# A four-layer convolution kernel: the last layer's spline taps stacked on output partitions and gathered two chunks later

## The reference

```
patches = _extract_patches(_gn(x), KSIZE, STRIDE, PAD)      # 3x3 windows
bspl = _b_splines(patches, grid)                            # 8 cubic B-splines of every value
base_w = base_weight.sum(axis=2)
spl_w = (spline_weight * spline_scaler[..., None]).sum(axis=2)
out = einsum('bjhwn,ijn->bihw', silu(patches), base_w)
out = out + einsum('bjhwns,ijns->bihw', bspl, spl_w) + bias
x = x + out
```

## Time and profile before

| what | us |
|---|---|
| median of 3 runs (lowest, highest) | 12135.7 (12120.45, 12162.18) |
| the profiled execution, its own time | 12114.81 |
| its span, first to last instruction | 12112.6 |
| TensorE busy over the span | 9570.5 |
| VectorE busy | 8958.4 |
| ScalarE busy | 7397.5 |
| GpSimd busy | 5088.7 |

### The profile page before, as it was taken

One profiled execution on the slowest core, in us unless ns is written; L12 is line 12 of the kernel. 1 busy time (PEld: TensorE's weight loads), 2 busy tenths in 40 slices (PEclk: granted clock), 3 DMA queues, 4 the chain that ended last, 5 costly groups with the idle time before them and its releaser, 6 DMA issues. The chain is left out here.

```text
span 12112.6 us, 205123 instructions
## 1 busy us (share of the span) xinstructions
PE 9570.5 (79%) x53055; PEld 4412.5 (36%) x53055; DVE 8958.4 (74%) x10913; ACT 7397.5 (61%) x10963; POOL 5088.7 (42%) x2442
## 2 busy tenths in 40 slices
PE   0788578857886788640199999999999999997599
PEld 0566456645664566510022222222222222222233
DVE  1778487847784787637488888888888888887677
ACT  0455345534553455324288888888888888886354
POOL 0233133312321233100166666666666666665243
PEclk9899789977997799875599999999999999999799
DMA  2000100010000000004311111111111111112544
GB/s 86 1 0 0 28 8 0 0 29 7 0 0 21 15 0 0 37 28 143 98 29 29 29 27 25 28 29 29 29 29 29 29 29 27 28 26 54 130 115 100
DMA packets 227136, 410.60 MB, mean 34 GB/s; under 512 B 28784, under 2 KB 163024, under 8 KB 212336
## 3 DMA queue, kind: packets, MB, share of 16 engines
q1 hardware_dynamic: 226150, 399.26, 12.9%
HBM read 283.44 MB, written 115.70 MB: 33 GB/s over the span
## 5 line engine op out<-in xcount | busy, mean ns | idle before, releaser
L1194 POOL TENSOR_TENSOR l_a<-l_a 128x1018 f32<-128x1018 f32 x1851 | 3453.3, 1883 | 1687.8 <-ACT l_a L1339 1673.0
L1309 DVE TENSOR_TENSOR l_r<-l_pps,l_a 128x509 f32<-128x509 f32 x4755 | 2989.0, 677 | 46.0 <-PE l_pps L1208 28.1
L1333 ACT ACTIVATE l_a<-l_qps 128x509 f32<-128x509 f32 x3705 | 2155.3, 596 | 818.4 <-PE l_qps L1208 566.0
L1339 ACT ACTIVATE l_a<-l_a 128x1018 f32<-128x1018 f32 x2380 | 2504.0, 1052 | 40.3 <-issue 40.3
L1208 PE MATMUL l_qps<-l_mv,l_wst 123*128 123x509 bf16 x4235 | 1644.6, 388 | 170.1 <-ACT l_a L1333 50.0
L1208 PE MATMUL l_pps<-l_mv,l_wst 123*128 123x509 bf16 x4228 | 1624.4, 384 | 63.6 <-DVE l_r L1309 60.9
L652 POOL TENSOR_TENSOR a_pr<-a_pr 128x768 f32<-128x768 f32 x384 | 898.4, 2340 | 1639.1 <-DVE a_pr L567 1624.0
L681 ACT ACTIVATE a_g<-a_fps 128x512 f32<-128x512 f32 x1152 | 680.4, 597 | 998.7 <-PE a_fps L434 997.3
L434 PE MATMUL a_fps<-a_hbt,a_wfc 96*128 96x512 f32 x2304 | 1222.2, 666 | 70.2 <-ACT a_g L681 70.2
L452 POOL TENSOR_TENSOR a_pr<-a_qkv 128x768 f32<-128x768 f32 x128 | 386.6, 3039 | 2089.3 <-ACT a_qkv L694 2089.3
L1297 DVE TENSOR_SCALAR l_a<-l_qps 128x509 int32<-128x509 int32 x1058 | 724.5, 685 | 688.2 <-PE l_qps L1208 677.6
(11 more groups left out here) (162 smaller groups left out, 12030.2 us busy)
## 6 DMA issues: line engine op xcount, KB each, us to landing
l_mv<-pw SPq DMA_DIRECT2D x1608, 79.5 KB
l_gx<-g SPq DMA_DIRECT2D x66, 1040.0 KB
pw<-pw_hi SPq DMA_DIRECT2D x165, 127.2 KB
pw<-pw_mid SPq DMA_DIRECT2D x165, 127.2 KB
pw<-pw_lo SPq DMA_DIRECT2D x165, 127.2 KB
a_tb<-g SPq DMA_DIRECT2D x16, 1031.9 KB
l_x<-x SPq DMA_DIRECT2D x16, 1024.0 KB, 12.1
l_gs<-g SPq DMA_DIRECT2D x33, 260.0 KB
```

The source lines that it names most:

```text
L1194: g.tensor_tensor(a, a, a, ALU.mult).then_inc(sq_p, 2)
L1309: v.tensor_tensor(R[:, m % R_RING, :], pps[:, m % P_BANKS, 0:SUB], A[:, m % A_RING, :], ALU.mult).then_inc(mul_done, 1)
L1333: s_.activation(A[:, s % A_RING, :], qps[:, s % Q_BANKS, 0:SUB], ACT.Abs).then_inc(abs_a, 1)
L1339: s_.activation(a, a, ACT.Abs_reciprocal_sqrt, bias=1.0).then_inc(root_done, 2)
```

## The change

Only `layer3` and its constants change. TensorE makes for each chunk k and each image j first a plane (`multiply`): 64 output partitions for each parity hold the three vertical taps dy (16 channels each) stacked, the two parities side by side, summed over the three horizontal taps dx. ScalarE (j = 0, 2) and VectorE (j = 1, 3) copy the planes from PSUM to SBUF (`keep`). Two chunks later (`gather`) a constant matrix `pick` adds the rows of the planes, shifted by dy, into the output bank. Silu's rows are paired: partitions 64 and up of `gs` hold the row below, so that one matmul makes taps dy = 0 and 1, another dy = 2, each for one half of the images. The first clamp becomes a `Relu` on ScalarE right behind `Abs`, the second goes to GpSimd, and the last sum of the two cubes goes from GpSimd to VectorE. In SyncE's queue the one `gs` load becomes six smaller ones into a single slot, issued one chunk later and behind a wait for the silu before; stores come two chunks later, and a `gx` slot is reloaded when `bases` is counted.

```diff
-GX, BSLOTS = 3, 3
+GX, BSLOTS, PSLOTS, PBANKS = 3, 2, 3, 6
+HALF = 2
+KEEP_DVE = {1, 3}
...
-                            for b in range(NB):
-                                last = v.tensor_scalar(wba[:, :, b, :], sw[:, 0, :, :], mask[:, b:b + 1], None, ALU.mult)
+                            for lo, both, dy in ((0, 0, 0), (64, 0, 1), (0, 1, 2)):
+                                for b in range(QUAD):
+                                    last = v.tensor_scalar(wba[lo:lo + 64, both, :, b, :], sw[lo:lo + 64, 0, 3 * dy:3 * dy + 3, :],
+                                                           mask[lo:lo + 64, b:b + 1], None, ALU.mult)
...
+                def load_silu(k):
+                    if k:
+                        sp.wait_ge(silu_done, k)
+                    for h in range(HALF):
+                        rows = g3[k].rearrange("e c j n -> j (e c) n")[2 * h:2 * h + 2]
+                        sp.dma_start(gs[0:64, h, :], rows).then_inc(gs_in, 16)
+                        sp.dma_start(gs[64:P, h, 0:CHN - QW], rows[:, :, QW:]).then_inc(gs_in, 16)
+                        if k + 1 < NCK:
+                            below = g3[k + 1].rearrange("e c j n -> j (e c) n")[2 * h:2 * h + 2, :, 0:QW]
+                            sp.dma_start(gs[64:P, h, CHN - QW:], below).then_inc(gs_in, 16)
...
                     if n >= GX:
-                        sp.wait_ge(b3_done, n - GX + 1)
+                        sp.wait_ge(bases, n - GX + 1)
...
-                    if e == 0:
-                        if k >= 2:
-                            sp.wait_ge(silu_done, k - 1)
-                        sp.dma_start(gs[:, k % 2, :], g3[k].rearrange("e c j n -> j (e c) n")).then_inc(gs_in[k % 2], 16)
-                    elif k >= 4:
-                        store(k - 4)
-                for k in range(NCK - 4, NOUT):
+                    if e == 0 and k:
+                        load_silu(k - 1)
+                    elif k >= 6:
+                        store(k - 6)
+                load_silu(NCK - 1)
+                for k in range(NCK - 6, NOUT):
                     store(k)
...
+            def silu_after(n):
+                return (n - 3) // PARITY if n >= 3 and n % PARITY else None
+            def kept_after(n):
+                return ((n - 3) // PARITY, (0, 1) if n % PARITY else (2, 3)) if n >= 3 else (None, ())
+            def finished_after(n):
+                return (n - 8) // PARITY if n >= 8 and n % PARITY == 0 and (n - 8) // PARITY < NOUT else None
...
+                    if n >= 2:
+                        act.wait_ge(a3_done, n - 1)
+                    s_.activation(na[:, n % 2, :], x, ACT.Relu, bias=two[:], scale=-1.0).then_inc(na_done, 1)
...
                 distance(0)
-                for n in range(NUNIT):
+                for n in range(NUNIT + 3):
                     if n + 1 < NUNIT:
                         distance(n + 1)
...
+                        s_.activation(b2[:], gx[:, n % GX, :], ACT.Square, scale=2.0).then_inc(b2_done, 1)
+                    k, js = kept_after(n)
+                    for j in js:
+                        if j not in KEEP_DVE:
+                            keep(act, lambda to, of: s_.activation(to, of, ACT.Copy), k, j).then_inc(plane_kept, 1)
+                    k = silu_after(n)
+                    if k is not None:
                         silu(k)
...
+                        v.tensor_tensor(B[:, e, :, at:at + CHN], gx[:, n % GX, :].rearrange("p (j n) -> p j n", j=QUAD),
+                                        a2[:, n % 2, :].rearrange("p (j n) -> p j n", j=QUAD), ALU.add).then_inc(bases, 1)
...
+                    x = gx[:, n % GX, :]
+                    pool.wait_ge(na_done, n + 1)
+                    nc.gpsimd.tensor_scalar(x, x, 1.0, 0.0, ALU.subtract, ALU.min).then_inc(nb_done, 1)
...
+                def multiply(k):
+                    pe.wait_ge(bases, PARITY * (k + 1))
+                    at = k % BSLOTS * CHN
+                    for j in range(QUAD):
+                        m = k * QUAD + j
+                        if m >= PBANKS:
+                            wait_kept(m - PBANKS)
+                        for dx in range(3):
+                            for e in range(PARITY):
+                                x = B[:, e, j, at:at + CHN].rearrange("p (r w) -> p r w", w=QW)[:, :, dx:dx + W]
+                                last = t.matmul(pps[64 * e:64 * e + 64, m % PBANKS, :].rearrange("p (r w) -> p r w", w=W), wsp[:, dx, :],
+                                                x, start=dx == 0, stop=dx == 2, skip_group_check=True)
+                        last.then_inc(plane_made, 1)
+                def gather(k):
...
+                    pe.wait_ge(silu_done, k + 2)
+                    for both, dy in ((0, 0), (1, 2)):
...
+                                for dx in range(3):
+                                    for h in range(HALF):
+                                        t.matmul(rows_out[64 * h:64 * h + 64, to_:to_ + n_, :],
+                                                 wba[:, both, dx, :, :].rearrange("p b f -> p (b f)"),
...
+                    wait_kept((k + 2) * QUAD - 1)
                     for dy in range(3):
                         for to, n, row in pieces(k, dy):
+                            for j in range(QUAD):
+                                last = t.matmul(rows_out[32 * j:32 * j + 32, to:to + n, :], pick[:, dy, :],
+                                                planes[:, j, row:row + n, :], start=False, stop=dy == 2, skip_group_check=True)
                     last.then_inc(o_made, 1)
+                for k in range(NCK):
+                    multiply(k)
+                    if k >= 2:
+                        gather(k - 2)
+                gather(NOUT - 1)
```

More of the change, by code:

```diff
@@ L1428, in _ @@
                     g = nc.gpsimd
+                    g.memset(two[:], 2.0).then_inc(zeroed, 1)
                     g.memset(wsp[:], 0.0).then_inc(zeroed, 1)
+                    g.memset(wba[:], 0.0).then_inc(zeroed, 1)
                     g.memset(G[:, 0, :], 0.0).then_inc(zeroed, 1)
@@ L1563, in finish @@
                     v.scalar_tensor_tensor(x, ops[:, k % 2, :], cbias[:], x, ALU.add, ALU.add).then_inc(o_done, 1)
[L1565 to L1576, removed]
@@ L1612, in _ @@
                     pe.wait_ge(silu_done, k + 2)
-                    silu = S[:].rearrange("p k (r w) -> p (k r) w", w=QW)
-                    first = True
+                    silu = S[:].rearrange("p k h (r w) -> p k h r w", w=QW)
+                    for both, dy in ((0, 0), (1, 2)):
+                        for to, n, row in pieces(k, dy):
+                            slots = [(to, n, row)]
+                            if row % CROWS + n > CROWS:
+                                cut = CROWS - row % CROWS
+                                slots = [(to, cut, row), (to + cut, n - cut, row + cut)]
+                            for to_, n_, row_ in slots:
+                                slot, r = divmod(row_, CROWS)
+                                for dx in range(3):
+                                    for h in range(HALF):
+                                        t.matmul(rows_out[64 * h:64 * h + 64, to_:to_ + n_, :],
+                                                 wba[:, both, dx, :, :].rearrange("p b f -> p (b f)"),
+                                                 silu[:, slot, h, r:r + n_, dx:dx + W], start=both == 0 and dx == 0, stop=False,
+                                                 skip_group_check=True)
@@ L1615, in _ @@
+                    wait_kept((k + 2) * QUAD - 1)
                     for dy in range(3):
                         for to, n, row in pieces(k, dy):
-                            for dx in range(3):
-                                t.matmul(rows_out[:, to:to + n, :], wba[:, 3 * dy + dx, :, :].rearrange("p b f -> p (b f)"),
-                                         silu[:, row:row + n, dx:dx + W], start=first, stop=False, skip_group_check=True)
-                                first = False
-                    for e in range(PARITY):
-                        pe.wait_ge(bases, PARITY * (k + 1) + e + 1)
-                        base = B[:, e].rearrange("p j (r w) -> p j r w", w=QW)
-                        for dy in range(3):
-                            for to, n, row in pieces(k, dy):
-                                for dx in range(3):
-                                    for j in range(QUAD):
-                                        last = t.matmul(rows_out[32 * j:32 * j + 32, to:to + n, :], wsp[:, e, 3 * dy + dx, :],
-                                                        base[:, j, row:row + n, dx:dx + W], start=False,
-                                                        stop=e == 1 and dy == 2 and dx == 2, skip_group_check=True)
@@ L1735, in lay_out @@
     got["w3_base"] = np.ascontiguousarray(np.broadcast_to(bw, (NB,) + bw.shape).reshape(P, 9, 9, C))
-    got["w3_mask"] = np.repeat(np.eye(NB, dtype=f32), C, axis=0)
```

(6 more changed lines are left out.)

114 lines of the change are left out of this document (66 added, 48 removed).

## The result

The changed kernel took 12,766.7 us (median of 4 runs, 12,733.4 to 12,787.9), the kernel before 12,128.1 us in the same series: a ratio of 1.0521, 95% interval 1.0487 to 1.0555. 12,908 was forecast, in a range of 12,600 to 13,030. The profiled execution took 12,787.9 us, its span 12,785.9.

What follows compares the result with a forecast made beforehand. TensorE was taken to pace the last layer, loads close second. Start 76, 31 chunks x 48.4 = 1500 and tail 34 gave 1610 us against 817.3: +793 on 12114.8 makes 12,908 us, range 12,600 to 13,030.

Steps and rivals of the forecast that it cites:

- TensorE paced the kernel before: Last layer before the change: TensorE always busy, 23.51 us a chunk; loads close second, filling 23.2 of 23.5 us.
- 21 passes instead of 27: TensorE, per chunk: 12 spline, 6 silu and 3 pick passes, 18.3 us against 23.5.
- SyncE's queue: gx(2m+3) stands behind six small loads waiting for silu m-1, so ScalarE idles 29.0 us; 48.4 us a chunk.
- Two DMA engines: Small silu loads: an outermost dimension of two j gives two engines, so 532 KB take 16.9 us.
- Start and tail: Last layer: 76 us until iteration 3 ends, and 34 us from the last bases to the span's end.
- The wait behind the small loads: ScalarE, from the end of silu to the use of gx(2m+3): 12.1 + 16.9 = 29.0 us idle a chunk.
- The second `gx` load: gx(2m+4), queued behind gx(2m+3), comes 9.8 us after it, longer than ScalarE's 8.5 us of work.
- GpSimd's clamp: Rival: clamp, taken as 3 us, outlasts its 11.7 us cover; up to 13,100. Chance 0.08 together with the half-clock rival.
- The half clock: Rival: TensorE's half clock delays gather, so ScalarE's copies wait; up to 13,100. Chance 0.08 together with the clamp rival.
- "The six saved passes count": Rival: loads keep ahead, wait falls under 4.2 us a chunk, pace 19 us; 11,970. Chance 0.05.

Runs made afterwards that it cites:

- run 10: The kernel before with only the gx load changed, its 16 channels made outermost (weights and distances permuted to match): 12,107 us (1.0000).
- run 2: The change with the six small loads issued behind a chunk's second gx load instead of ahead of it, wait for silu unchanged: 12,457 us (1.0275).
- run 6: The change with the small loads of chunk m issued behind gx(2m+4) instead of ahead of gx(2m+3): 12,384 us (1.0230).
- run 3: The change with the six small loads cut into twelve, 32 rows outermost instead of 2, same bytes and waits: 12,558.6 us (1.0358).
- run 4: The change with the gx load's 16 channels outermost and its eight copies inner, same bytes and queue: 12,624 us (1.0413).
- run 7: The change with small loads issued late as in run 6, 32 pairs outermost in them, and gx as in run 4: 12,118 us (0.9998).
- run 11: The change with small loads and gx spread over all DMA engines as in run 7, but in the change's queue order: 12,323 us (1.0169).
- run 5: The change with the second clamp back on VectorE and the last sum back on GpSimd: 12,720 us (1.0507).
- run 8: As run 7, with the second clamp on VectorE and the last sum on GpSimd: 12,094 us (0.9988).
- run 9: As run 8, with a fourth gx slot; the second square is written to the buffer the first product has just finished with: 12,185 us (1.0047).
- run 12: As run 9, with VectorE's clamp of the next unit moved behind the first product: 12,103 us (0.9988).

## Why the prediction was right, point by point

**TensorE paced the kernel before**: run 10 shows it. The loads filled 23.2 of 23.5 us, and with a faster `gx` (the first one used 7.8 us after its issue instead of 12.1) nothing was gained but at the start, while TensorE's chain stayed at 23.51 us a chunk.

**21 passes instead of 27**: right, 18.6 us. Worth nothing in the change, since TensorE idles half the time.

**SyncE's queue**: right, and shown in several ways. Its order alone takes 309 us (run 2) or 383 us (run 6) off; the engines of the small loads alone take 208 (run 3), those of `gx` 142 (run 4). Runs 7 and 11 close a square: neither 12,767, late order alone 12,384, fast loads alone 12,323, both 12,118. The two gains of 383 and 444 overlap to 649, as both shorten the same wait and another bound lies below.

**Two DMA engines**: a share of 0.13 in the window of small loads. By the rule of the Trainium skill ("DMA: Bandwidth & Descriptors", section "Why a DMA increments its semaphore by 16 and not by 1"), two is the largest number that divides the 2 of the source and the 64 partitions. The trace agrees; and where the same bytes come with 32 rows outermost the time falls, by 208 us.

**The sizes.** A chunk took 43.8 us in the mean (silu from 11386.60 to 12745.01 in 31 chunks) and 44.9 in the one shown, against 48.4. Start and tail were 72.7 and 39.8 us, against 76 and 34. The overshoot of 139 us is 31 x 4.6 in the chunks. The mechanism was right, and two terms were too large. The wait behind the small loads was 26.86 us in the chunk shown and 25.9 in the mean, against 29.0: 44 GB/s on two engines while they are alone, where I had halved 63 to 31.5. The second `gx` load: I let it come 9.8 us after the first, but ScalarE, 8.1 us later, did not wait for it at all. Both loads end on the two late engines, and these move 26.5 GB/s each there (53 / 2, by that reading), against 13.4 (107 / 8) in the earlier trace rows.

**GpSimd's clamp.** My upper bound was wrong: 7.27 us, not 1.7 to 4.67. The cover of 11.7 us held it, so the rival did not come in that form. Beside it VectorE's first products took 3.72 and its sums 4.25 us in the mean, and `Relu` waited about 0.8 us a chunk for VectorE (25.0 us, 31 times). Moving the clamp back shortened the block by 32.3 us in one profile (run 5); the timings do not separate this from nothing.

**The half clock.** The passes of `pick` ran at a granted clock of 0.50 and took 5.35 us instead of 2.79, but ScalarE's copies waited for TensorE only twice in the block, 16.1 us in all. This rival did not come.

**"The six saved passes count"**: the rival's condition was that the wait fall under 4.2 us a chunk. In run 7 the `Abs` behind silu waits 1.9 us in the mean and the other one 3.7. So the condition held, yet the time is the same as before and not 11,970: that the rest would then run at 19 us was wrong. Three slots that are held until the last sum, with ScalarE one unit ahead, limit a chunk to 22 to 23 us. This is argued from the rounds in runs 7 and 8 and supported by runs 9 and 12, where the wait for `gx` is gone; no run has four slots without the serial square. In the profiled executions the second block took 795.8 us in run 8 against 817.3 in the kernel before. The whole kernel's time can't tell the two apart, since the start of the block alone differs by up to 50.8 us among the profiled executions. Whether the change could clearly beat the kernel before stays open.

## What to carry to other kernels

In a queue that issues in order, a load that waits for a late event delays every load behind it. Find the last event of each wait and ask which engine wants the next load at that very time; a spare slot does not help there. Look at the outermost dimension of each DMA's source before splitting it into halves: here 2 rows outermost meant an eighth of the engines. And when passes are saved on the pacing engine, first list the other rounds (slots times the time one is held): here a saving of 5 us a chunk stood over rounds of 22 to 23.

## What the runs showed of the hardware

- A one-input `tensor_scalar` (subtract, min) on GpSimd took 7.27 us for 128x2080 float32, longer than its two-input sum (4.67). The Trainium skill ("GPSIMD Engine Reference", section 4.1 "Engine selection") calls one-input operations roughly line-rate; this measurement differs, and it decides.
- While it ran, VectorE's two-input operations, 2.3 us alone, took 4.91 and 6.57. Beside GpSimd's two-input sum a one-input clamp of VectorE, 1.24 us alone, took 5.53 (run 10).
- A DMA engine moved 26.5 GB/s of a `gx` load when two of them were at work on it (53 GB/s at a share of 0.12), and 13.4 when all eight were (107 GB/s at 0.50).
